# Attention on one Trainium2 core: the order of work in a slot, and the PSUM banks under it

## The reference, cut to what matters

```python
# x: (4, 1024, 256); kernel: (3, 16 heads, 256, 64); WO: (1, 1024, 256)
q = einsum('bsm,hmd->bhsd', x, kernel[0])
k = einsum('bsm,hmd->bhsd', x, kernel[1])
v = einsum('bsm,hmd->bhsd', x, kernel[2])
attn = softmax(einsum('bhsd,bhtd->bhst', q, k) / (64 * 64 * 16), axis=-1)
out = einsum('bhst,bhtd->bhsd', attn, v)            # then transposed, reshaped and times WO
x = layernorm(x + attention)
x = layernorm(x + moe(x))    # 8 experts, 2 of them per token, a shared layer, another layernorm
```

## Time and profile before

| | us |
|---|---|
| median of 3 runs | 1949.17 (1947.44 to 1950.61) |
| the profiled execution, its own time | 1948.51 |
| its span, first to last instruction | 1946.7 |

### The profile page before, as it was taken

One profiled execution on the slowest core, in us unless ns is written; L12 is line 12 of the kernel. 1 busy time (PEld: TensorE's weight loads), 2 busy tenths in 40 slices (PEclk: granted clock), 3 DMA queues, 4 the chain that ended last, 5 costly groups with the idle time before them and its releaser, 6 DMA issues. The chain is left out here.

```text
span 1946.7 us, 31549 instructions
## 1 busy us (share of the span) xinstructions
PE 1835.3 (94%) x11161; PEld 1202.2 (62%) x11161; DVE 1351.5 (69%) x1772; ACT 1019.2 (52%) x1490; POOL 353.2 (18%) x399
## 2 busy tenths in 40 slices
PE   7999999999999999999999999788747999999986
PEld 5555545455554545455554544487737999999982
DVE  5777777777677777777777787755564666666646
ACT  5555555554555555555555555454445555555537
POOL 1000000000000000000000000001115777776764
PEclk9999999999999999999999999898968999999998
DMA  5000000000000000300000000154221333334335
GB/s 167 17 28 17 23 17 28 22 17 28 17 23 17 28 19 21 111 17 22 17 28 17 23 22 17 67 206 152 98 112 36 90 86 86 86 86 88 87 51 173
DMA packets 67089, 110.29 MB, mean 57 GB/s; under 512 B 7712, under 2 KB 41696, under 8 KB 64672
## 3 DMA queue, kind: packets, MB, share of 16 engines
q1 hardware_dynamic: 48704, 81.48, 12.4%
q0 software_dynamic: 18272, 27.31, 7.0%
HBM read 70.20 MB, written 38.57 MB: 56 GB/s over the span
## 5 line engine op out<-in xcount | busy, mean ns | idle before, releaser
L430 ACT ACTIVATE a_e<-banks 128x1024 f32<-128x1024 f32 x512 | 496.7, 1022 | 350.9 <-PE banks L318 350.9
L530 DVE TENSOR_TENSOR a_esum<-a_esum,a_e 128x1024 f32<-128x1024 f32 x384 | 469.6, 1223 | 129.0 <-ACT a_e L430 105.4
L334 PE MATMUL banks<-a_e,a_v 128*64 128x512 f32 x2048 | 495.7, 605 | 0.0
L334 PEld LDWEIGHTS banks<-a_e,a_v 128*64 128x64 f32 x2048 | 124.2, 136 | 238.2 <-issue 167.1
L318 PE MATMUL banks<-a_qh,a_kh 64*128 64x512 f32 x1024 | 229.7, 445 | 5.2 <-issue 5.2
L534 DVE RECIPROCAL a_inv<-banks 128x512 f32<-128x512 f32 x64 | 214.9, 3358 | 15.4 <-PE banks L345 15.4
L63 POOL MEMSET ident<- 128x128 f32 x1 | 0.2, 204 | 1219.9 <-POOLq L109 1219.9
L318 PEld LDWEIGHTS banks<-a_qh,a_kh 64*128 64x128 f32 x1024 | 95.9, 184 | 196.0 <-issue 129.7
L318 PE MATMUL banks<-a_ql,a_kh 64*128 64x512 f32 x1024 | 201.8, 391 | 0.0
L318 PE MATMUL banks<-a_qh,a_kl 64*128 64x512 f32 x1024 | 201.6, 390 | 0.0
L1738 ACT ACTIVATE e_g<-banks,e_b1c 128x256 f32<-128x256 f32 x280 | 116.4, 471 | 144.2 <-PE banks L1685 143.5
(11 more groups left out here) (226 smaller groups left out, 3270.7 us busy)
## 6 DMA issues: line engine op xcount, KB each, us to landing
attn_out<-a_ot SPq DMA_DIRECT2D x64, 256.0 KB, 2.0
a_w<-w_qkv SPq DMA_DIRECT2D x32, 256.0 KB, 3.1
raw<-attn_out SPq DMA_DIRECT2D x4, 2048.0 KB, 8.1
t_ot<-attn_out SPq DMA_DIRECT2D x4, 2048.0 KB, 7.9
raw<-w_up SPq DMA_DIRECT2D x8, 1024.0 KB, 5.0
raw<-w_down SPq DMA_DIRECT2D x8, 1024.0 KB
raw<-x_t SPq DMA_DIRECT2D x8, 512.0 KB, 9.3
x_rows<-x POOLq DMA_DIRECT2D x7, 512.0 KB, 3.4
```

The lines of the kernel that those rows point to most:

```text
L334: mm = pe.matmul(o_acc[slot % 2][h * DH:(h + 1) * DH, :], v[quad % 2][:, n, head], e[n % NE][:, h * BANK:(h + 1) * BANK], start=n == 0, st ...
L430: act.activation(e[n % NE], ring[n % 2], ACT.Exp, scale=SCALE).then_inc(e_ok, 1)
L530: dve.tensor_tensor(acc[:, :], acc[:, :], e[n % NE], ALU.add).then_inc(add_ok, 1)
```

## The change

The score ring gets a third place of two banks (banks 0 to 5), so the eight key tiles go in groups of three, three and two. On TensorE a slot becomes: S0 S1 S2, the last two V of the slot before and its sums, S3 S4 S5, V0 V1 V2, S6 S7, the units, V3 V4 V5. The Q and K units take the two banks of the ring's third place, which the group of two leaves free. The V unit takes the bank of the row sums (`side`, bank 7). One output accumulator is left (bank 6): ScalarE copies it to SBUF (`o_raw`) when the slot's last V is done, V0 of the next slot waits for that copy, and VectorE's multiply reads it. There are six `e` tiles instead of four. ScalarE and VectorE follow the same grouping: VectorE takes the reciprocal after two adds of the slot instead of one, and the low parts of Q and K after the slot's last add instead of after the fifth; the splitting of weights and x comes a group earlier.

```diff
-    NE = 4
+    NE = 6
-        ring, o_acc, sum_ps, proj = banks.both[0:2], banks[4:6], banks[6], banks[7]
+        ring, o_acc, side = banks.both[0:3], banks[6], banks[7]
+        GROUPS = [range(0, 3), range(3, 6), range(6, ST)]
 def unit_out(u):
-            return (proj, sum_ps, o_acc[(slot - 1) % 2])[k]
+            return side if k == 2 else ring[RING - 1][:, k * BANK:(k + 1) * BANK]
 def pe_unit(pe, u):
-                if k == 0 and slot:
-                    wait_evacuated(pe, units(slot - 1)[0])
-                elif k and slot:
-                    pe.wait_ge((inv_ok, o_ok)[k - 1], slot)
+                if k < 2:
+                    pe.wait_ge(e_ok, slot * ST + ST - 2)
+                elif slot:
+                    pe.wait_ge(inv_ok, slot)
 def scores(slot, n):
-                if t >= 2:
+                if n >= RING:
+                    pe.wait_ge(e_ok, t - RING + 1)
+                elif slot and n < RING - 1:
                     pe.wait_ge(e_ok, t - 1)
+                elif slot:
+                    for u in units(slot - 1)[0:2]:
+                        wait_evacuated(pe, u)
 def values(slot, n):
-                    if slot >= 2:
-                        pe.wait_ge(o_ok, slot - 1)
-                    if slot and len(units(slot - 1)) > 2:
-                        wait_evacuated(pe, units(slot - 1)[2])
+                    if slot:
+                        pe.wait_ge(o_copied, slot)
 def sums(slot):
-                if len(units(slot)) > 1:
-                    wait_evacuated(pe, units(slot)[1])
+                if len(units(slot)) > 2:
+                    wait_evacuated(pe, units(slot)[2])
 TensorE, for each slot:
-                for j in range(ST // 2):
-                    scores(slot, 2 * j)
-                    scores(slot, 2 * j + 1)
+                for j, group in enumerate(GROUPS):
+                    for n in group:
+                        scores(slot, n)
+                    for u in units(slot) if j == 2 else ():
+                        pe_unit(pe, u)
                     if j:
-                        values(slot, 2 * j - 2)
-                        values(slot, 2 * j - 1)
-                        for u in todo if j == VISIT else ():
-                            pe_unit(pe, u)
+                        for n in GROUPS[j - 1]:
+                            values(slot, n)
                     elif slot:
-                        values(slot - 1, ST - 2)
-                        values(slot - 1, ST - 1)
+                        for n in GROUPS[-1]:
+                            values(slot - 1, n)
                         sums(slot - 1)
 ScalarE:
+            def output(slot):
+                act.wait_ge(pv_done, slot * ST + ST)
+                if slot:
+                    act.wait_ge(o_ok, slot)
+                act.copy(o_raw[:, :], o_acc).then_inc(o_copied, 1)
+                for j, group in enumerate(GROUPS):
+                    for n in group:
+                        probs(slot, n)
+                    if j == 0 and slot:
+                        output(slot - 1)
+                    if j == 0 and m == 0 and i + 2 < B * PAIRS:
+                        act_weights(act, i + 2)
+                    if j == 1 and m == 0 and ...:
+                        act_rows_high(...)
+                    for u in units(slot) if j == 2 else ():
+                        act_evacuate(act, u)
 VectorE:
 def normalize(slot):
-                dve.wait_ge(pv_done, slot * ST + ST)
+                dve.wait_ge(o_copied, slot + 1)
-                dve.tensor_tensor(ot[slot % 2][:, :], o_acc[slot % 2], inv[:, :], ALU.mult)
+                dve.tensor_tensor(ot[slot % 2][:, :], o_raw[:, :], inv[:, :], ALU.mult)
+                for j, group in enumerate(GROUPS):
+                    for n in group:
+                        if n:
+                            add(slot, n)
                     if j == 0 and slot:
                         normalize(slot - 1)
+                    if j == 0 and m == 0 and i + 2 < B * PAIRS:
+                        dve_weights(dve, i + 2)
+                    if j == 1 and m == 0 and ...:
+                        dve_rows_low(...)
+                    for u in units(slot) if j == 2 else ():
+                        dve_evacuate(dve, u)
```

More of the change, by code:

```diff
@@ L132, in attention @@
         ot = [sb(f"a_ot{u}", [P, BANK]) for u in range(2)]
+        o_raw = sb("a_o_raw", [P, BANK])
         ones = sb("a_ones", [P, DH])
@@ L161, in attention @@
             sem("a_" + n) for n in ("s_done", "e_ok", "add_ok", "pv_done", "sum_done", "inv_ok", "o_ok"))
+        o_copied = sem("a_o_copied")
         ot_out = keep["ot_out"]
         Q, K, V = range(3)
-        VISIT = 2
+        RING = 3
+        GROUPS = [range(0, 3), range(3, 6), range(6, ST)]
         FIRST_BANKS = 6
@@ L310, in scores @@
                 t = slot * ST + n
-                if t >= 2:
+                if n >= RING:
+                    pe.wait_ge(e_ok, t - RING + 1)
+                elif slot and n < RING - 1:
                     pe.wait_ge(e_ok, t - 1)
-                tile, cols, keys = ring[n % 2], slice(m * BANK, (m + 1) * BANK), slice(n * P, (n + 1) * P)
+                elif slot:
+                    for u in units(slot - 1)[0:2]:
+                        wait_evacuated(pe, u)
+                tile, cols, keys = ring[n % RING], slice(m * BANK, (m + 1) * BANK), slice(n * P, (n + 1) * P)
                 high, low = qk_h[i % 2], qk_l[i % 2]
@@ L333, in values @@
                     head = slice(pair * P + h * DH, pair * P + (h + 1) * DH)
-                    mm = pe.matmul(o_acc[slot % 2][h * DH:(h + 1) * DH, :], v[quad % 2][:, n, head],
-                                   e[n % NE][:, h * BANK:(h + 1) * BANK], start=n == 0, stop=n == ST - 1)
+                    mm = pe.matmul(o_acc[h * DH:(h + 1) * DH, :], v[quad % 2][:, n, head],
+                                   e[(slot * ST + n) % NE][:, h * BANK:(h + 1) * BANK], start=n == 0, stop=n == ST - 1)
                 mm.then_inc(pv_done, 1)
@@ L341, in sums @@
                     pe.wait_ge(inv_ok, slot)
-                if len(units(slot)) > 1:
-                    wait_evacuated(pe, units(slot)[1])
+                if len(units(slot)) > 2:
+                    wait_evacuated(pe, units(slot)[2])
                 for h in range(2):
-                    mm = pe.matmul(sum_ps[h * DH:(h + 1) * DH, :], ones[:, :], esum[slot % 2][:, h * BANK:(h + 1) * BANK],
+                    mm = pe.matmul(side[h * DH:(h + 1) * DH, :], ones[:, :], esum[slot % 2][:, h * BANK:(h + 1) * BANK],
                                    start=True, stop=True)
@@ L350, in pe_bounded @@
             for slot in range(SLOTS):
-                todo = units(slot)
-                for j in range(ST // 2):
-                    scores(slot, 2 * j)
-                    scores(slot, 2 * j + 1)
+                for j, group in enumerate(GROUPS):
[3 more added lines that the diff above has]
+                        pe_unit(pe, u)
                     if j:
-                        values(slot, 2 * j - 2)
-                        values(slot, 2 * j - 1)
-                        for u in todo if j == VISIT else ():
-                            pe_unit(pe, u)
+                        for n in GROUPS[j - 1]:
+                            values(slot, n)
                     elif slot:
-                        values(slot - 1, ST - 2)
-                        values(slot - 1, ST - 1)
+                        for n in GROUPS[-1]:
+                            values(slot - 1, n)
                         sums(slot - 1)
@@ L429, in probs @@
                     act.wait_ge(add_ok, before * ADDS + max((t - NE) % ST, 1))
-                act.activation(e[n % NE], ring[n % 2], ACT.Exp, scale=SCALE).then_inc(e_ok, 1)
+                act.activation(e[t % NE], ring[n % RING], ACT.Exp, scale=SCALE).then_inc(e_ok, 1)
+            def output(slot):
[3 more added lines that the diff above has]
+                act.copy(o_raw[:, :], o_acc).then_inc(o_copied, 1)
             for slot in range(SLOTS):
                 i, m = slot // NB, slot % NB
[L434 to L438, removed]
+                for j, group in enumerate(GROUPS):
[5 more added lines that the diff above has]
+                        act_weights(act, i + 2)
+                    if j == 1 and m == 0 and i % PAIRS in (1, 2) and i // PAIRS + 1 < B:
+                        act_rows_high(act, 2 * (i // PAIRS + 1) + i % PAIRS - 1)
+                    for u in units(slot) if j == 2 else ():
                         act_evacuate(act, u)
[L440 to L443, removed]
+            output(SLOTS - 1)
         def dve_rows_low(dve, j):
@@ L526, in add @@
                         dve.wait_ge(sum_done, slot - 1)
-                    dve.tensor_tensor(acc[:, :], e[0], e[1], ALU.add).then_inc(add_ok, 1)
+                    dve.tensor_tensor(acc[:, :], e[(t - 1) % NE], e[t % NE], ALU.add).then_inc(add_ok, 1)
                 else:
```

(14 more changed lines are left out.)

## The result

The changed kernel takes 1924.68 us (median of 4 runs, 1923.85 to 1925.81) against 1948.31 us for the kernel before on the same chip: a ratio of 0.9877, 95% interval 0.9862 to 0.9892. It is 24 us faster; 1928 us, 20 us faster, was forecast. A later measurement gave 0.9873 (0.9858 to 0.9888).

What follows compares the result with a forecast made beforehand. TensorE, busy for all 1201.81 us of attention, was taken as the bound. 63 x 0.35 = 22.0 us, plus 0.1, less 1.2, takes 20.9 from 1948.51: 1927.6, median 1928.3, predicted 1928 us, range 1917 to 1941.

Steps and rivals of the forecast that it cites:

- A round less, 0.35 us each: TensorE in attention: three score-and-value rounds per slot instead of four save one fixed cost of 0.35 us.
- The units' new place costs what the old one did: TensorE, units between S7 and V3: the place costs 0.19 us beside the units' steps, as before S6.
- Rivals 1 and 2: Units' place: first, fp32r passage from scores free, 1916 us, chance 0.07; second, place dear at 0.38 us, 1940 us, 0.09.
- The new waits don't bite: Steady slots: ScalarE's copy, exponentials and VectorE's list finish in time; the low part of K has 1.1 us to spare.
- Slots 56 to 61 lose 1.2 us: Shorter two-unit slots: VectorE's low part of K comes 0.4 us late in slots 57, 59 and 61, 1.2 us lost.
- The end: Last slot of attention: VectorE's adds end it, so it gains 0.1 us instead of 0.35.
- The sum: All attention slots: 63 x 0.35 = 22.0 us, plus 0.1, less 1.2, a gain of 20.9 us.
- Rival 3: TensorE's rounds: the fixed cost belongs to per-tile waits or fresh reads, so fewer rounds save nothing; 1949 us, chance 0.05.
- Rival 4: VectorE's low part of K, moved later, delays the next S0; 1965 us at a lag of 2.1 us, chance 0.05.

Runs made afterwards that it cites:

- experiment 1: Changed kernel with groups of two again, four rounds per slot, everything else kept: 1948.73 us, ratio 1.0002 to the kernel before.
- (4): Changed kernel with the units between S6 and S7, and S0 waiting for only the first half of the keys: 1951.56 us, ratio 0.9941 to the kernel before.
- experiment 9: Changed kernel with two groups of four, eight e tiles, relaxed S0 wait, x split behind the units' evacuation: 1906.14 us, ratio 0.9782 to the kernel before.
- experiment 2: Changed kernel with the units placed between S6 and S7: 1962.29 us, ratio 1.0072 to the kernel before.
- experiment 10: Changed kernel with the V unit's matmuls in fp32 instead of fp32r, same operands and shape: 2135.8 us, one run.
- experiment 5: Changed kernel with one useless 128x1024 add on VectorE behind each slot's last add: ratio 0.9915 to the kernel before.
- experiment 6: Changed kernel with two useless 128x1024 adds on VectorE behind each slot's last add, each waiting for the one before: ratio 1.0154 to the kernel before.
- experiment 8: Changed kernel with two groups of four, eight e tiles, units in order Q, K, V, relaxed S0 wait: ratio 0.9798 to the kernel before.

## Why the prediction was right, and where its sizes were off

- **A round less, 0.35 us each.** Right. The slot fell from 19.01 to 18.645 us (mean of the distances, each 18.64 or 18.65), 0.365; experiment 1 puts the round back and gets 19.01 again. The price goes with the number of changes of shape. Without waits the slot is 19.01 us at nine changes (before, and experiment 1), 18.81 at eight (4), 18.645 at seven, 18.32 at five (9): 0.16 to 0.18 us per change. Between the two fp32r kinds, where the type stays, the shape alone costs: in experiment 2 scores, units and scores again lose 0.2 us against the changed kernel's block (8.83 against 8.63). From V to fp32r scores or units, both change: the V group is 0.16 us longer than its tiles, while the passage from units to scores is 0.08 longer than a step. Whether the 0.08 between them belongs to the type or to the 64 columns is not shown. By the rule that the prediction drew from the Trainium skill, TensorEngine Tiling (Array Packing), Key Properties, a change of tiling mode, not just of the tile, drains TensorE. The price per change agrees with it in every one of these kernels, and so does the V unit in experiment 10, which changed its type and not its mode; that the time is spent draining is seen in none of them.
- **The units' new place costs what the old one did.** Right: 4.31 against 4.34 us, the passage to V 0.32 (704.55 to 704.87) against 0.31 to S6. Rivals 1 and 2 fall; the last score matmul of S7 to the first unit takes 0.33 us (700.23 to 700.56) and not 0.23. That the fp32r passage from scores to units is not free is seen in experiments 2 and 4 as well, 0.16 us for going there and back instead of on to the values.
- **The new waits don't bite.** Right in all steady slots. The accumulator's copy ended at +4.85 (forecast +5.0), the reciprocal started at +5.45 (5.7), the low part of K ended at +17.2 (17.6). VectorE was early because the reciprocal started 0.08 us before the add ahead of it ended (694.40, with that add from 693.25 for 1.23), and the low part of K 0.60 after that of Q, not 0.69.
- **Slots 56 to 61 lose 1.2 us: wrong.** They take 17.28 us. The last row of VectorE and the weight load that waited for it, in slot 59:

```profile
1148.88 0.68 DVE L481 TENSOR_TENSOR a_kl<-banks,a_kh 128x512 fp32r<-128x512 f32 x1
...
1149.67 0.19 PEld L326 LDWEIGHTS banks<-a_qh,a_kh 64*128 64x128 f32 x2 [0.81 <-DVE a_kl L481]
```

  The low part of K ends at 1149.56 and S0 starts at 1149.67, with the 0.81 us of idle load time that every S0 has. The 0.4 us by which VectorE was ahead of my layout were all that this needed.
- **The end.** S0 to the sums took 16.03 us against 16.35, a gain of 0.3 where 0.1 was forecast.

```profile
1198.59 0.50 PE L326 MATMUL banks<-a_qh,a_kh 64*128 64x512 f32 x2
...
1214.62 1.08 PE L351 MATMUL banks<-a_esum,a_ones 128*64 128x512 f32 x4
```

- **The sum.** Forecast 20.9 us in attention, measured 1200.73 - 1177.16 = 23.57 (first score to last sums). The difference of 2.7 is one of sizes, all to the same side: 1.2 for the short slots, 63 x 0.015 = 0.9 for the round, 0.2 for the last slot, 0.2 in slot 0, which gained 0.52; the hundredths of the rows hold the rest. The opening was 0.54 us longer in this execution and what follows attention 0.57 shorter. The median of 1924.68 lies 3.6 us below the forecast's 1928.3; the other 0.9 us is that the forecast put the median 0.66 above the profiled execution, and it came out 0.24 below it.
- **Rival 3** fell with experiment 1: the same tiles and the same waits per tile, one round more, and the whole gain is gone.
- **Rival 4, VectorE's low part of K.** Its mechanism is real and its margin small. The forecast had it decide from 1.1 us on in odd slots; it was 1.48, and experiment 5 shows that 1.33 pass, experiment 6 that 2.66 turn the gain into a loss. Its least expected form was the units' place: before S6 or between S6 and S7 they lose 57 or 38 us against the changed kernel, nearly all of the 57, and 29 of the 38 by the slots of experiments 2 and 4, because the low part of K then comes too late; the rest of the 38 is the eighth change of shape. The forecast laid VectorE's list out for the new place only. It had costed the old one by TensorE's blocks alone.

## What to carry to other kernels

Where one engine's list is full, count what happens between its groups: subtract the groups' steps from the distance between their starts, and count the kinds that meet. Fewer, longer runs of one shape are worth the PSUM and the SBUF that they take, down to the point where the engine behind can't free a place in time; read that point from its starts, tile by tile, not from its rate, since a group of four went through three places without a wait. And when work is moved, lay out the slowest list that ends in a wait, not only the one that is full: moving the same matmuls by one tile cost 38 us here, 29 of them through a list that is busy for three quarters of the time.

## What was not expected of the hardware

- An fp32 matmul of 128 rows and 128 columns takes 0.86 us, and so does a pair of 64-column ones side by side: the 0.855 us of a V tile is one full matmul's time.
- A semaphore from VectorE to TensorE was answered in 0.05 us (705.05 to 705.10, 729.98 to 730.03).
- The same program took 15 us longer on one of three chips (1963.47 against 1948.57 and 1948.84 us for the kernel before). The slots did not. From the last row sums to the end the four kernels profiled on the slow chip (experiments 4, 5, 6 and 8) take 722.9 to 724.0 us, all others 705.0 to 709.4. Part of it is seen from 303 to 603 us behind those sums: TensorE is busy for 96 to 99% of that stretch in experiment 8, on the slow chip, and for 99.8% in experiment 9, at a granted clock of 1.00 in both. What holds it there was not looked for.
